# Swapping gather and scatter on TensorE in a graph network's message sums

## The reference

```python
row, col = edge_index[0], edge_index[1]          # src, dst
for t in range(2):
    src, dest = x[row], x[col]
    m_input = jnp.concatenate([dest, src, edge_attr], axis=1)
    messages = m_input @ msg_W[t].T + msg_b[t]
    agg = jax.ops.segment_sum(messages, row, num_segments=x.shape[0])
    x = _gru_cell(agg, x, gru_Wih[t], gru_bih[t], gru_Whh[t], gru_bhh[t])
```

## Time and profile before

| what | us |
|---|---|
| median of 3 runs | 2308.71 |
| lowest, highest | 2308.26, 2317.59 |
| the profiled execution | 2315.87 |
| its span, first to last instruction | 2314.3 |
| mean granted TensorE clock | 0.99 of full |

### The profile page before, as it was taken

How to read it: one execution, slowest core, us unless ns; L and a number is a source line. 1 busy time by engine, 2 the same in 40 slices (tenths; PEclk the granted TensorE clock), 3 DMA queues, 4 the chain that set the end, 5 groups by cost and what they waited for, 6 DMA issues and landing times. The chain is left out here.

```text
span 2314.3 us, 120470 instructions
## 1 busy us (share of the span) xinstructions
PE 1511.9 (65%) x43734; PEld 1408.6 (61%) x43734; DVE 2132.0 (92%) x3390; ACT 1896.1 (82%) x4474; POOL 734.8 (32%) x1245
## 2 busy tenths in 40 slices
PE   0000000000024889999999999968999999999996
PEld 0000000000013889999999999858899999999995
DVE  6999999999967879999999999958999999999995
ACT  4678795664124879999999999958999999999996
POOL 1000000000085546666666666522122112222221
PEclk9999999999999999999999999989999999999998
DMA  5200000211133656667676777637666777777773
GB/s 100 56 0 0 0 0 17 64 22 22 53 93 84 215 183 231 225 225 233 225 231 225 229 229 231 221 109 242 222 239 241 238 240 240 238 239 242 240 241 113
DMA packets 165547, 376.03 MB, mean 162 GB/s; under 512 B 70854, under 2 KB 87404, under 8 KB 164792
## 3 DMA queue, kind: packets, MB, share of 16 engines
q1 hardware_dynamic: 114299, 191.07, 26.4%
q0 software_dynamic: 49456, 181.94, 24.0%
q10 hardware_dynamic: 1708, 1.97, 0.3%
HBM read 358.39 MB, written 16.17 MB: 162 GB/s over the span
## 5 line engine op out<-in xcount | busy, mean ns | idle before, releaser
L1387 ACT ACTIVATE rows<-ps_rows 128x512 f16<-128x512 f32 (+1 forms) x2744 | 1362.8, 610 | 64.4 <-PE ps_rows L1286 54.4
L1491 DVE TENSOR_TENSOR src<-iota_units,src_lane 128x2048 f16<-128x2048 f16 (+2 forms) x784 | 801.0, 1022 | 37.6 <-PE ps_sum L1306 19.3
L1308 PE MATMUL ps_sum<-rows,src 128*64 128x132 f16 x10192 | 556.4, 222 | 17.1 <-issue 9.1
L1286 PE MATMUL ps_rows<-rows_next,planes 128*64 128x128 f16 x10192 | 536.7, 219 | 36.5 <-DVE planes L1487 22.9
L1286 PE MATMUL ps_rows<-rows_now,planes 128*64 128x128 f16 x10192 | 545.4, 219 | 20.9 <-ACT rows L1387 9.0
L1306 PE MATMUL ps_sum<-src,rows 128*64 128x128 f16 x10192 | 543.3, 221 | 6.1 <-issue 2.1
L1487 DVE TENSOR_SCALAR planes<-planes,lane_no 128x2048 f16<-128x2048 f16 (+2 forms) x784 | 514.2, 656 | 11.4 <-DMA planes<-lanes_dram 11.1
L804 PE MATMUL ps_src<-ident,late 104*64 104x104 f32 x98 | 19.9, 380 | 641.5 <-DVE late L1039 622.9
L1286 PEld LDWEIGHTS ps_rows<-rows_now,planes 128*64 128x64 f16 x10192 | 411.9, 110 | 42.6 <-ACT rows L1387 16.6
L1286 PEld LDWEIGHTS ps_rows<-rows_next,planes 128*64 128x64 f16 x10192 | 398.2, 109 | 58.8 <-DVE planes L1487 23.5
L1308 PEld LDWEIGHTS ps_sum<-rows,src 128*64 128x64 f16 x10192 | 397.1, 110 | 25.3 <-ACT rows L1387 17.9
(11 more groups left out here) (213 smaller groups left out, 2187.4 us busy)
## 6 DMA issues: line engine op xcount, KB each, us to landing
planes<-lanes_dram POOLq DMA_DIRECT2D x196, 512.0 KB, 4.4
planes<-lanes_dram SPq DMA_DIRECT2D x194, 512.0 KB, 4.5
planes<-lanes_dram POOLq DMA_DIRECT2D x98, 448.0 KB, 4.7
planes<-lanes_dram SPq DMA_DIRECT2D x97, 448.0 KB, 4.6
planes<-lanes_dram POOLq DMA_DIRECT2D x98, 192.0 KB, 3.8
planes<-lanes_dram SPq DMA_DIRECT2D x97, 192.0 KB, 3.7
rows_now<-parts_dram SPq DMA_DIRECT2D x104, 32.0 KB, 1.7
rows_next<-parts_dram SPq DMA_DIRECT2D x104, 32.0 KB, 3.9
```

The costliest lines, as they stand in the source:

```text
L1286: last = nc.tensor.matmul(ps_rows[(u + NU * b) % 4][half * SLOTS:(half + 1) * SLOTS, k * 2 * H:(k + 1) * 2 * H], dst1[q][:, (c - 2 * QUART ...
L1308: last = nc.tensor.matmul(ps_sum[b][at, 0:width], hot[:, at], row, start=(j == 0), stop=(j == J - 1))
L1387: nc.scalar.activation(rows_of_unit(u, b)[:, :, 0:2 * H], cut(ps_rows[(u + NU * b) % 4][:])[:, 0:n, :], ACT.Copy).then_inc(rows_ready, 1)
L1491: nc.vector.tensor_tensor(src1[q][:], iota_units[:].rearrange("p (o l) k -> p o l k", o=1) .broadcast_to([P, pairs_now, P, 2]), src_lane[: ...
```

## The change

In the body of a tile on PE, the scatter of the unit three behind is issued ahead of the unit's gather. Turn, gates and the extras' transposes stay behind both. It holds for both rounds.

```diff
@@ -1355,13 +1355,13 @@
                     def body(s, b, half):
                         later_tile = past(s, 1)
                         for u in range(NU):
-                            gather(s, u, b)
-                            if flipped and not later_tile and u == TURN_AT:
-                                turn_extras()
                             if u >= LAG:
                                 scatter(s, u - LAG, b)
                             elif later_tile:
                                 scatter(s - 1, NU - LAG + u, 1 - b)
+                            gather(s, u, b)
+                            if flipped and not later_tile and u == TURN_AT:
+                                turn_extras()
                             if past(s, 2) and u == TURN_AT:
                                 turn(s - 2, b)
                             if past(s, 2) and u == GATES_AT:
```

## The result

The changed kernel takes 2364.54 us (median of 3, 2361.75 to 2366.77) against 2308.71: ratio 1.0237, 95% interval 1.0216 to 1.0259. It is slower by 56 us, where 60 were forecast (2369, range 2334 to 2405).

A forecast was written before the change was run, and what follows sets the result against it. In the second round PE, closely coupled to ACT's copies, was taken as the bound; in the first, DVE. Second round +37 and first +23, other terms 0, gave 2308.7 + 60 = 2369 us, range 2334 to 2405.

The forecast's parts named there:

- The mechanism: Gather to scatter on PE falls from 1.60 to 1.14 us; ACT's copy needs 1.15, so the 0.45 us cushion goes.
- The long run: Units after gates, S(6) to S(9): ACT's copies finish 0.49 us apart, making PE wait 0.20 us a tile.
- the sigmoid's stall: S(9) in the odd tile waits 0.26 us behind ACT's sigmoid; with the long run's 0.20, 0.46 for that tile.
- The short units: Six-matmul units late in a tile: waits up to 0.19 us, taken as 0.15 in the even tile.
- The loop's turn: PE's hole of 0.38 us between tile pairs, held to be the loop's own cost and unchanged.
- +0.76 a pair: Second round: 0.66 us of added waits plus 0.1 for restarts, over 49 pairs +37 us.
- The first round: DVE paces pairs at 15.5 us against PE's 15.2, covering 0.3 of 0.76; 49 x 0.46 = +23 us.
- The signs named beforehand: Periods 15.5 and 16.0 us, ACT-attributed idle before L1306 over 30, longer DVE waits, PE near 95%, clock 1.00.
- DVE and POOL at nothing: Src buffers come free one step (0.22 us) earlier, but later PE gives DVE and POOL none of it: 0.
- ACT alone as the bound: Rival: ACT's 14.4 of 14.77 us a pair sets the pace, so time stays at 2309, within 5; chance 0.08.
- A faster kernel by earlier src builds: Rival: DVE limits the second round and gets scatters a step earlier, saving 12 us: 2297; chance 0.04.
- The clock: Rival: more waits lower the granted clock to 0.88 throughout, giving 2510 us; chance 0.02.

The follow-up runs named there:

- experiment 1: The changed kernel (scatter first) with the scatter of the unit four behind, not three: 2302.53 us, ratio 0.9949 to the kernel before.
- experiment 2: The kernel before (gather first) with the scatter of the unit two behind, not three: 2426.31 us, ratio 1.0487.
- experiment 9: The changed kernel with the scatter of the unit two behind, not three: 2785.19 us, ratio 1.2043 to the kernel before.
- experiment 3: The kernel before with ACT copying only 64 of each 128 columns of a gather, the other half zero: 2285.91 us, ratio 0.9881.
- experiment 4: The changed kernel with ACT copying only 64 of each 128 columns of a gather, the other half zero: 2293.75 us, ratio 0.992.

## Why the prediction was right, point by point

**The mechanism** held: distance 1.60 to 1.14, ring of three. Experiments 1, 2 and 9 turn it off, on and up by the lag alone, experiments 3 and 4 by the take's length.

**The long run** ("the next ones 0.49 apart", waits of 0.20 in a tile) is what the trace of the even tile shows: 0.49 between scatters, and from S(5) to S(9) 1.96 us (1906.08 to 1908.04) where two full and two mixed units need 0.46 + 0.46 + 0.40 + 0.40 = 1.72, so 0.24. In the odd tile it is not there: S(5) to S(8) is 1.38 us (1898.23 to 1899.61) for 1.32. There the sigmoid's stall was taken too small instead, 0.26 for a measured 0.34, so the walk's 0.46 for the tile came near the measured 0.4 partly by luck.

**The short units** were mis-sized: I took 0.15 and they cost 0.05. S(11) to G(0) has 0.22 for 0.17; ACT's short copies come fast enough:

```profile
1908.63 0.34 PE L1286 MATMUL ps_rows<-rows_next,planes 128*64 128x128 f16 x6
1908.80 0.36 PE L1306 MATMUL ps_sum<-src,rows 128*64 128x128 f16 x6
1909.02 0.41 PE L1286 MATMUL ps_rows<-rows_next,planes 128*64 128x128 f16 x8
```

**The loop's turn** is the step that failed: "this is the loop's turn on PE, and the change leaves it". It went from 0.38 to 0.16 at the same loop code, 0.2 us a pair given back, some 9 us in the second round. (The loop turns 44 times a round and not 49, as its first ten tiles are unrolled.) I had rightly seen that the row's releaser was long done, and wrongly concluded that the rest was a constant; the branch rows of experiment 3 show that it depends on how far PE's sequencer is ahead. These two errors are most of what makes the second round's +0.76 a pair into the measured +0.51 (25 us for 37).

**The first round** erred the other way: +0.63 a pair for +0.46, 31 us for 23. DVE's pace is 15.46, as five kernels show, and before the change the pair took 15.52; after it the pair takes 16.15, so DVE no longer paces it, and I missed a term. In the first round only, ACT's copy L1423 stands ahead of the sigmoid. The changed kernel's odd tile, ACT and then PE:

```profile
1312.80 0.31 ACT L1423 ACTIVATE new_parts<-h 128x128 f16 x1
1312.99 0.60 ACT L1387 ACTIVATE rows<-ps_rows 128x512 f16<-128x512 f32 x1
1313.47 0.40 ACT L1417 ACTIVATE rz<-ps_gates 128x256 f32<-128x256 f32 x1
```

```profile
1313.22 0.33 PE L1286 MATMUL ps_rows<-rows_now,planes 128*64 128x128 f16 x6
1313.65 0.42 PE L1308 MATMUL ps_sum<-rows,src 128*64 128x132 f16 x8
1313.91 0.33 PE L1286 MATMUL ps_rows<-rows_now,planes 128*64 128x128 f16 x6
1314.41 0.43 PE L1308 MATMUL ps_sum<-rows,src 128*64 128x132 f16 x8 [0.17 <-ACT rows L1387]
```

There are two stalls, 0.43 and 0.50 for 0.17 each, one behind L1423 and one behind the sigmoid. Before the change the cushion swallowed the first. So the total of 60 against 56 owes something to luck, to errors of opposite sign: 37 and 23 forecast, 25 and 31 measured.

**The signs named beforehand** came in part. The periods are 15.25 and 16.15 us for 15.5 and 16.0, DVE waits longer and the clock stayed. The idle time before L1306 rose from 9.0 to 39.3 us, but of that only 16.6 is put down to ACT, where over 30 was named; and PE's busy share did not fall to 95% but rose to 99%, though it did fewer matmuls: the share was no sign to go by.

**DVE and POOL at nothing** held for the change: DVE's scatters come a step earlier in the order, and its waits for them grew all the same.

**The rivals.** ACT alone as the bound: no, it fell from 99% to 98% busy in the second round and went idle before takes, 9.4 us in 550 for 2.8; experiment 3 shows that the kernel before had been waiting for it all the same. A faster kernel by earlier src builds: no. The clock: 1.00 throughout. For ACT's rate the measured 0.48 to 0.49 us carried the walk, and the trace bears it out: scatters of the long run are 0.49 apart. The estimate of 519 ns worked out from the Trainium skill, page ScalarE: Activation LUTs, section What ACT_TABLE_LOAD costs, would have put them 0.52 apart; here the measurement decides.

## What to carry to other kernels

In a software pipeline over several engines, write for each handover the time between producer and consumer in the issuing engine's own order, and what has to fit into it; an order that keeps every lag in units can still take away two steps of seven. If the steps are swapped, raise the lag by one: here that turned 2.4% slower into 0.5% faster. Put the steps that let the slow engine catch up ahead of the first step that needs its late result, and look for small waits from start to start, since the list of waits shows only the long ones.

## What I had not expected of the hardware

The hole at the turn of PE's loop is 0.38 us when PE has just waited for ACT and 0.02 when it has not, at the same instructions: the branch takes 0.21 us on PE's sequencer in both, and only its start against the array's work differs. And doubling the body of that loop moved instruction fetches from 0.75 to 7.19 MB and the time from 2309 to 2888 us, with waits for issue of up to 7.6 us and a lower granted clock: here the size of the loop's body mattered far more than its number of turns.
